# A relational graph layer: x in two 12-bit parts as fp32r words against masks spread to words by ScalarE, in place of three bf16 parts against fp8 masks

## What is computed

```python
rel_ids = jnp.arange(1, 5)                                  # four relations
masks = (relation[None] == rel_ids[:, None, None, None])    # relation is adj
h = jnp.einsum('rbnm,bmd->rbnd', masks, x)
y = jnp.einsum('rbnd,rdo->bno', h, weight) + bias           # weight (4,128,128)
out = layernorm(x + y, axis=-1)                             # eps 1e-5, no gain
```

## Time and profile before

| what | value |
|---|---|
| runs of the kernel | 136.88 us median of 3 (136.84 to 136.92) |
| the profiled execution's own time | 135.64 us |
| its span | 133.9 us |
| busy: PE, DVE, ACT, POOL | 119.4, 100.2, 78.4, 71.5 us |
| read from HBM, written to it | 37.88 MB, 4.19 MB |

### The profile page before, as it was taken

The page is one execution under the profiler, slowest core; times in us unless marked ns, Lnnn a source line. Parts: engine busy times, 40 slices in busy tenths (PEclk is TensorE's granted clock), DMA queues, the critical chain, the costliest instruction groups (busy, mean ns, idle before and its releaser), DMA issues.

```text
span 133.9 us, 2116 instructions
## 1 busy us (share of the span) xinstructions
PE 119.4 (89%) x675; PEld 73.2 (55%) x675; DVE 100.2 (75%) x274; ACT 78.4 (59%) x81; POOL 71.5 (53%) x79
## 2 busy tenths in 40 slices
PE   5884879949979999999999999999999999999920
PEld 4553668714526474746464646464656555567810
DVE  1487333177429999999999897969699999967871
ACT  3004862682699786959494949494949494123050
POOL 3000009950903995599379919990964559705260
PEclk9999999995999999999999999999999999999997
DMA  4999969999999999999999999999961200300322
GB/s 109 415 436 423 416 237 423 421 431 412 427 423 420 417 411 426 416 421 423 415 422 411 428 414 423 418 421 415 411 279 54 109 0 5 126 31 0 159 78 86
DMA packets 7788, 42.23 MB, mean 315 GB/s; under 512 B 864, under 2 KB 1376, under 8 KB 3936
## 3 DMA queue, kind: packets, MB, share of 16 engines
q1 hardware_dynamic: 7776, 42.08, 76.8%
HBM read 37.88 MB, written 4.19 MB: 314 GB/s over the span
## 4 chain that ended last, share of the span: by engine, by line
PE 63%; DMA 16%; ACT 5%; SPq 5%; DVE 5%; issue 2%; POOL 2%; POOLq 0%; DVEq 0%; ACTq 0%
PE h_ps L212 49%; DMA adj_sb<-in_adj_dram 16%; PE y_ps L219 9%; PE tp_ps L191 5%; ACT mask L183 4%; SPq L164 2%; POOL scale L237 2%; SPq L279 1%; DVE paired L492 1%; DVE stats L225 1%; SPq L167 1%; DVE total L509 1%; ACT h_sb L416 0%; DVE mean_var L230 0%; DVE out_sb L241 0%
## 5 line engine op out<-in xcount | busy, mean ns | idle before, releaser
L183 ACT ACTIVATE mask<-adj_sb 128x2048 fp8e3<-128x2048 int32 x30 | 55.9, 1902 | 14.3 <-DMA adj_sb<-in_adj_dram 14.3
L212 PE MATMUL h_ps<-maskT,x_sb 128*128 128x512 fp8e4 (+1 forms) x152 | 32.9, 359 | 3.5 <-DVE maskT L199 2.9
L212 PE MATMUL h_ps<-maskT,x_fine 128*128 128x512 fp8e4 (+1 forms) x152 | 32.0, 352 | 0.4 <-DVE x_fine L176 0.4
L212 PE MATMUL h_ps<-maskT,x_rest 128*128 128x512 fp8e4 (+1 forms) x152 | 32.2, 353 | 0.0
L179 POOL TENSOR_TENSOR x_bias<-x_sb,bias_sb 128x1024 f32<-128x1024 f32 x8 | 21.3, 2660 | 18.1 <-DMA bias_sb<-in_L_gnn_bias_dram 18.1
L199 DVE TENSOR_SCALAR maskT<-tp_ps 128x512 uint32<-128x512 uint32 x30 | 19.4, 683 | 11.4 <-PE tp_ps L191 11.4
L492 DVE SCALAR_TENSOR_TENSOR paired<-mask 128x512 uint32<-128x512 uint32 x13 | 20.3, 1562 | 6.6 <-ACT mask L183 6.1
L212 PEld LDWEIGHTS h_ps<-maskT,x_sb 128*128 128x128 bf16 x152 | 14.4, 97 | 19.0 <-DVE maskT L199 3.3
L356 POOL TENSOR_SCALAR minus_mean<-mean_var 128x4 f32<-128x4 f32 (+1 forms) x16 | 3.1, 195 | 37.2 <-DVE var_eps L234 21.4
L212 PEld LDWEIGHTS h_ps<-maskT,x_rest 128*128 128x128 bf16 x152 | 14.8, 98 | 11.5 <-DVE x_rest L173 0.3
L212 PEld LDWEIGHTS h_ps<-maskT,x_fine 128*128 128x128 bf16 x152 | 14.6, 96 | 11.8 <-DVE x_fine L176 0.7
(11 more groups left out here) (31 smaller groups left out, 63.8 us busy)
## 6 DMA issues: line engine op xcount, KB each, us to landing
adj_sb<-in_adj_dram SPq DMA_DIRECT2D x30, 1024.0 KB, 18.2
x_sb<-in_x_dram SPq DMA_DIRECT2D x8, 512.0 KB, 18.2
out_dram<-out_sb SPq DMA_DIRECT2D x7, 512.0 KB, 12.9
adj_sb<-in_adj_dram SPq DMA_DIRECT2D x4, 512.0 KB, 5.2
out_dram<-out_sb SPq DMA_DIRECT2D x1, 256.0 KB, 2.0
out_dram<-out_sb SPq DMA_DIRECT2D x2, 128.0 KB, 1.9
bias_sb<-in_L_gnn_bias_dram SPq DMA_DIRECT2D x1, 64.0 KB, 14.7
w_sb<-in_L_gnn_weight_dram SPq DMA_DIRECT2D x1, 64.0 KB, 14.5
```

The costliest lines, as they stand in the source:

```text
L183: nc.scalar.activation(mask[:, slot % NMASK].bitcast(code), adj_sb[:, slot % NADJ], ACT.Copy, scale=CODE, saturate=False).then_inc(done, 1)
L212: last = nc.tensor.matmul(h_ps[:, bank, 0:n], x_t, m_t, start=(part == 0 and t == 0), stop=(part == PARTS - 1 and t == TILES - 1))
```

## The change

- x is cut into two parts instead of three. `top` on VectorE masks x to its upper 12 significant bits (one `bitwise_and` over 1024 words); GpSimd copies that to the fp32r tile `x_hi`, and subtracts it from x into the fp32r tile `x_lo`. For batch 0 ScalarE makes the copy and VectorE the difference.
- The masks are fp32r words. VectorE makes the bytes of a unit (`convert`: min with 2, times 60, int32 to uint8, where 60 is the fp8e5 code of 1.0 and 120 that of 32768), TensorE transposes the words of every unit (no pairs), and ScalarE reads the four bytes of a word out of PSUM as fp8e5 and writes them as fp32r (`expand`, 2048 elements), with the sum of each row as a second result (`counts`), from which the flag is made in the end. The ORs, evacuations and pairs of VectorE are gone.
- The bias is no longer added to x. It is cut into three bf16 parts in three rows of a tile; one product of ones with that tile opens the accumulation of y (`spread_bias`), and the residual x is added straight from `x_sb`.
- The pieces of the first two units are gone; all units are whole, and h is copied unscaled. Four x slots (5 before), four `maskT` slots (6 before, four times as wide now). SP issues three small bias loads and the weight right after unit 1. 12 warm-up products, in bf16.

```diff
-        def convert_chunk(slot, done):
-            nc.scalar.activation(mask[:, slot % NMASK].bitcast(code), adj_sb[:, slot % NADJ], ACT.Copy, scale=CODE,
...
+        def take_top(x_slot, done):
+            nc.vector.tensor_scalar(flat(x_top[:, :]), flat(x_sb[:, x_slot]).bitcast(u32), TOP_BITS, None,
+                                    ALU.bitwise_and).then_inc(done, 1)
+        def take_lo(eng, x_slot, slot, done):
+            eng.tensor_tensor(flat(x_lo[:, slot]), flat(x_sb[:, x_slot]), flat(x_top[:, :]).bitcast(fp32),
+                              ALU.subtract).then_inc(done, 1)
+        def part_products(part, slot, places, bank, first, last_part):
+            n = (places.stop - places.start) * OP
             for t in range(TILES):
+                last = nc.tensor.matmul(h_ps[:, bank, 0:n], (x_hi, x_lo)[part][:, slot, t, :],
+                                        maskT[:, places, t // WORD, t % WORD, :],
+                                        start=(first and t == 0), stop=(last_part and t == TILES - 1))
...
+        def spread_bias(y, tiles):
+            n = tiles.stop - tiles.start
+            nc.tensor.matmul(y[:, 0:n, :], spread[:, :], bias_parts[:, 0:n, :], start=True, stop=False)
...
# SP
+            def load_batch(b):
                 if b >= NX:
+                    sp.wait_ge(added, CH * (b - NX + 1))
...
# POOL
             for b in range(B):
                 if b + 1 < B:
-                    rest(b + 1)
+                    hi(b + 1)
                 if b >= 1:
                     scales_half(2 * b - 1)
                 if b + 1 < B:
-                    fine(b + 1)
-                    bias_on(b + 1)
+                    lo(b + 1)
                 scales_half(2 * b)
...
# ACT
+            def expand(u):
+                act.wait_ge(turned, u + 1)
+                if u >= NMT:
+                    act.wait_ge(multiplied, u - NMT + 1)
+                nc.scalar.activation(maskT[:, u % NMT], turned_codes(u % NTP), ACT.Copy,
+                                     accum_out=counts[:, u:u + 1]).then_inc(expanded, 1)
...
+            for hf in range(HALVES - 1):
+                if hf >= 1:
+                    copy_half(hf - 1)
+                expand(2 * hf + 2)
+                expand(2 * hf + 3)
+                if hf >= 2:
+                    finish_half(hf - 2)
...
# DVE
+            def convert(u):
+                dve.wait_ge(adj_loaded[u % NADJ], 16 * (u // NADJ + 1))
+                if u >= NMASK:
+                    dve.wait_ge(turned, u - NMASK + 1)
+                nc.vector.tensor_scalar(mask[:, u % NMASK], adj_sb[:, u % NADJ].bitcast(u32), CAP, SET,
+                                        ALU.min, ALU.mult).then_inc(masked, 1)
...
+            for hf in range(HALVES - 1):
+                for u in (2 * hf + 5, 2 * hf + 6):
+                    if u < UNITS:
+                        convert(u)
+                if hf % 2 == 0 and hf // 2 + 1 < B:
+                    top(hf // 2 + 1)
+                if hf >= 1:
+                    add_half(hf - 1)
+                    measure_half(hf - 1)
+                if hf >= 2:
+                    finish_half(hf - 2)
...
# PE
+            turn(0)
+            turn(1)
             turn(2)
+            for hf in range(HALVES - 1):
+                if 2 * hf + 3 < UNITS:
+                    turn(2 * hf + 3)
+                hi_products(hf)
+                if 2 * hf + 4 < UNITS:
+                    turn(2 * hf + 4)
...
+                if hf >= 1:
+                    project_half(hf - 1)
+                lo_products(hf)
             products_quarter(HALVES - 1, 0)
             project_half(HALVES - 2)
+            products_quarter(HALVES - 1, 1)
             project_quarter(HALVES - 1, 0)
```

More of the change, by code:

```diff
@@ L13 @@
 CH = 4
[L14 to L19, removed]
+SET = 60.0
+CAP = 2.0
+FULL = 2048.5
+TOP_BITS = 0xFFFFF000
 def relational_layer(nc, x, adj, weight, bias, out):
-    fp32, bf16, fp8 = mybir.dt.float32, mybir.dt.bfloat16, mybir.dt.float8e4
-    code = mybir.dt.float8e3
-    i32, u32 = mybir.dt.int32, mybir.dt.uint32
+    fp32, fp32r, bf16 = mybir.dt.float32, mybir.dt.float32r, mybir.dt.bfloat16
+    code = mybir.dt.float8e5
+    i32, u32, u8 = mybir.dt.int32, mybir.dt.uint32, mybir.dt.uint8
     ALU, ACT, AX = mybir.AluOpType, mybir.ActivationFunctionType, mybir.AxisListType
@@ L218, in project @@
                 for r in range(relations):
[L219 to L220 removed]
+                    last = nc.tensor.matmul(y[:, n, :], h_of(r)[:, s], w_sb[:, r, :], start=False,
+                                            stop=(r == relations - 1 and s == tiles.stop - 1))
             last.then_inc(done, by)
@@ L456, in _ @@
                 with act.Fori(0, B) as b:
-                    with act.Fori(0, R) as r:
+                    for r in range(R):
                         for half in range(2):
+                            for ch in (2 * half, 2 * half + 1):
+                                k = CH * R * b + CH * r + ch
+                                act.wait_ge(g_turned, k + 1)
+                                if r > 0:
+                                    act.wait_ge(g_multiplied, 2 * R * b + 2 * r + half - 1)
+                                nc.scalar.copy(act_scratch[:, CH * r + ch + 1:CH * r + ch + 2], act_scratch[:, 0:1])
+                                nc.scalar.activation(maskT[:, ch], turned_codes(ch % NTP), ACT.Copy).then_inc(g_expanded, 1)
                             act.wait_ge(g_multiplied, 2 * R * b + 2 * r + half + 1)
@@ L496, in empty_pair @@
[L496 to L503 removed]
+            nc.vector.memset(act_scratch[:, :], 0.0).then_inc(scratch_set, 1)
@@ L504, in add @@
+            def add(b, y, tiles, count, by):
                 dve.wait_ge(projected, count)
-                dve.wait_ge(biased, b + 1)
-                if hf % 2 == 0 and b >= NTOTAL:
+                if b >= NTOTAL:
                     dve.wait_ge(act_normed, CH * (b - NTOTAL + 1))
-                tiles = slice(HT * (hf % 2) + O * c_slice.start, HT * (hf % 2) + O * c_slice.stop)
-                nc.vector.tensor_tensor(total[:, b % NTOTAL, tiles], y, x_bias[:, b % 2, tiles], ALU.add).then_inc(added, by)
+                nc.vector.tensor_tensor(total[:, b % NTOTAL, tiles], y, x_sb[:, b % NX, tiles], ALU.add).then_inc(added, by)
@@ new lines, in place_bias @@
+            def place_bias():
+                dve.wait_ge(bias_split, 3)
+                for q, part in zip(PARTS, (bias_rows, bias_rest, bias_fine)):
+                    last = nc.vector.tensor_copy(bias_parts[q:q + 1], upper(part[q:q + 1, :]).unsqueeze(1).to_broadcast(
+                        [1, HT, D]))
+                last.then_inc(bias_split, 1)
+            convert(0)
+            top(0)
+            convert(1)
+            dve.wait_ge(topped, 1)
+            take_lo(nc.vector, 0, 0, lo_made)
@@ L689, in products_quarter @@
                 place = (2 * hf + c) % NMT
-                wait_chunk(pe, piece_evacuated, evacuated, 2 * hf + c)
-                for part in range(PARTS):
-                    if hf % 2 == 0 and c == 0:
-                        x_ready(part, b)
-                    last = part_products(part, b % NX, b % 2, slice(place, place + 1), bank_of(hf, c))
-                last.then_inc(multiplied, 1)
+                pe.wait_ge(expanded, 2 * hf + c + 1)
+                part_products(0, b % 2, slice(place, place + 1), (hf + c) % NBANK, True, False)
+                part_products(1, b % 2, slice(place, place + 1), (hf + c) % NBANK, False, True).then_inc(multiplied, 1)
             def keep_warm(times):
```

443 lines of the change are left out of this document (145 added, 298 removed).

## The result

The changed kernel took 127.46 us, median of 4 runs (126.66 to 128.38); the kernel before took 136.86 beside it. The ratio is 0.9315, with the 95% interval [0.9244, 0.9385]: faster by 6.2 to 7.6%, and 6.3 us slower than the 121.2 predicted, inside its range. The execution that was profiled took 128.38 us, the longest of the four, 1.78 more than its span of 126.6.

The account below looks back on a forecast made before the run. TensorE was taken as the bound, at 5.82 us a half: start to 35.0, 11 halves to 99.0, end 19.2, span 118.2, plus 1.74 and 1.24 gave 121.2 us; range 116.5 to 130.

Parts of the forecast that it names:

- Rivals 3 and 4: Third: `convert` runs at the single rate, 143 us, chance 0.07. Fourth: an fp32r product still takes 427 ns, 167 us, chance 0.04.
- VectorE's own work: VectorE's operations per half without collisions, from two `convert` and half a `top` to the last normalisation: 5.44 us.
- VectorE against GpSimd: VectorE operations waiting out GpSimd's `lo`, expected at the second `convert` of odd iterations: 0.4 us a batch, bounds 0 and 1.9.
- TensorE with 0.08 for jostling: Pace of the late halves: TensorE's 5.74 us plus 0.08 for coupled engines, 5.82 us a half.
- Rival 1: Locks between VectorE and GpSimd, or ScalarE, set the pace: 7.0 us a half, 131 us; at 6.3, 126; chance 0.23.
- S14: Time TensorE starts half 14 (S with a number: start of that half), predicted at 99.0 us.
- S3: Time TensorE starts half 3, predicted at 35.0 us; from there halves were to follow 5.82 us apart.
- ScalarE and start: ScalarE 5.5 us a half, with `expand` 1.93; TensorE's first half begins at 15.8 us, 1.7 to 2 slower for its clock.
- the sign of being wrong: DMA, expected near 420 GB/s to 93 us: a dip would put SP's wait on the path.
- SP's new wait: A load of x waits for the sums of the batch four before; taken to cost nothing.
- End: From half 14's start on TensorE to the end of the span: 19.2 us with small waits, giving a span of 118.2.
- my own case: TensorE bounds the whole kernel: 5.65 to 6.1 us a half, 119.5 to 124.5 us, held at 0.57.

Follow-up runs that it names:

- E9: E6 with ScalarE normalising three of a half's four row tiles and VectorE one, up to half 11; 120.88 us.
- E1: The changed kernel with eps added to the variance on GpSimd instead of VectorE; 127.17 us.
- E7: The changed kernel with GpSimd making each `x_lo` of batches 1 to 7 twice, the first into a tile nobody reads; 138.56 us.
- E6: The changed kernel with TensorE's general loop over relations rolled again and ScalarE normalising a half one iteration later; 123.66 us.
- E8: The kernel before the change, with TensorE's general loop over four relations written as four copies; 139.27 us.
- E4: The changed kernel with TensorE's general loop, which doesn't run, looping over the relations again instead of four copies; 124.36 us.

## Why the prediction was right, and where it was wrong

The change is faster, as forecast, and the time lies in the range. The bound that the prediction named for the new kernel, TensorE, was wrong: it is VectorE with a stall behind GpSimd, and that the time came out near is in part luck.

**TensorE: right.** Eight fp32r products take 1.86 us, 233 ns each (230 taken); transposes 0.46, bias product 0.22, projection 0.89. Sum 2 x 1.86 + 2 x 0.46 + 0.22 + 0.89 = 5.75 (5.74 predicted), which is just the pace of E9. Rivals 3 and 4 fell: a convert is 1.22, an fp32r product far from 427. The Trainium skill (SBUF — State Buffer, "A bandwidth-pool intuition that's wrong") gives TensorE's moving operand 2 bytes a lane and cycle at 2.4 GHz, for bf16. An estimate from that figure puts 512 columns of 4-byte words at 427 ns; the measured 233 decides against this reading of it.

**VectorE's own work: right.** 5.44 a half predicted, 10.69 / 2 = 5.35 found.

**VectorE against GpSimd: the step that failed.** I took 0.4 us a batch for the collision and kept 0 and 1.9 as bounds; it is 1.32, in nearly every batch. Two things in it were wrong. `x_lo` was priced at the 1.90 of L176 but takes 2.40: it has two fp32 inputs, as the bias add of the kernel before has, whose mean was 2.66. And I looked for the collision at the converts only, arguing that they stand in line already. All but one do; the one that is hit is the small addition of eps before them, then by E1 and E7 the normalisation. 10.69 + 1.32 makes 6.0 a half against TensorE's 5.75, so the bound changed its engine: "TensorE with 0.08 for jostling" was the wrong mechanism with a number, 5.82, near the right 6.0. Rival 1, that the locks set the pace, was the right one in its milder form: with 6.3 a half it gave S14 at 104 and 126 us. (Its 109 to 110 for 7.0 a half is a slip, 35.0 + 11 x 7.0 is 112.)

**The other way round, L550 was the right guide.** GpSimd's short power never stretched a convert, so rival 1 in its full form (7.0 a half) did not come. But I costed GpSimd at 1.5 for a half's scales, "it bounds nothing", and did not ask what its wait does to those behind it: a power took 3.3 to 3.9 us with two or three double-rate operations of VectorE beside it, so `shift` was late, ScalarE waited 19.8 us for it, and an expand behind that came later. E6 puts this at 1.2 us.

**What it adds up to at S14**, +5.4: 0.4 at S3; 2.0 for pace (5.5 batches of 12.0 instead of 11.64); and 3.0 more between S3 and S7, at 62.4, where a half took 6.75 rather than 6.0. Of these 3.0, 1.2 fall on the first half alone, 35.40 to 42.63, where TensorE waits for a convert of VectorE (TensorE, then VectorE):
```profile
42.63 0.74 PE L178 MATMUL tp_ps<-identity,mask 128*128 128x128 f32 x4 [0.73 <-DVE mask L426]
```
```profile
41.36 2.36 DVE L426 TENSOR_SCALAR mask<-adj_sb 128x2048 uint8<-128x2048 uint32 x2
```
That convert stands in VectorE's order behind a `top`, an add, statistics and a normalisation, from 38.05 on. The loads had let TensorE work 2.65 us ahead of VectorE's `top` (35.4 against 38.05), and I had not counted that this lead must be given back once VectorE sets the pace; by S7 TensorE stood 0.5 behind (62.4 against 61.88), where it stayed. E9 has this first half too (35.29 to 42.39) and then goes on at 5.8. Another 1.2 is ScalarE's order (E6). The last 0.6 stays open.

**ScalarE and start: right.** Expand 1.87 (1.93 taken), the row sum an instruction of its own of 197 ns, mostly overlapped (0.1 taken); reading every fourth byte cost nothing; `hi` 1.04 (1.5 taken). The start came within 0.4 us, with the granted clock at 0.50, the 1.2 GHz level, from 10.3 to 20.5 us, after TensorE had little to do from 7 us on; I had put 1.7 to 2 us on the first half for it, and the loads covered it.

**DMA: the sign of being wrong came, its cause was another.** I had said that a dip would put SP's new wait on the path. There are dips, to 365, 359 and 281 GB/s in single slices, and 400 in the mean. But they go when VectorE gets less to do, with the same four x slots: E9 has 420 in the mean and, but for the first and the last slice of the loads, none under 404, while E6, which differs from it in that alone, still dips to 341 and 320. So they follow from a late VectorE, which frees the slots.

**End: a term was missing.** From S14 to the last normalisation 16.8 for 16.6. (The terms given add up to 13.8 + 5.5 = 19.3, and the prediction has 19.2 with small waits; it matters little.) Then 5.4 instead of 2.6, as the branch takes 4.05 us where it took 0.37. The line was in the diff; I read it as code that doesn't run. Code that doesn't run had a price of 2.6 us in E8; in E4 2.7 of the 4.0 that the span lost are of the end.

**The sum.** The span was 126.6 for 118.2 predicted, +8.4: 5.4 at S14, 0.2, and 2.8 for the branch. The profiled execution was 0.9 above the median where I had put it 1.24 below, which by chance takes 2.1 back: 6.3 in the time. With the loop rolled (E4) the kernel stands at 124.3, inside the 119.5 to 124.5 of my own case, but with VectorE as the bound and not TensorE.

## What to carry to other kernels

Where VectorE and GpSimd both work out of SBUF, add to VectorE's own sum that part of each long GpSimd operation under which VectorE has no statistics to take (1.3 of 2.4 us here, 2.2 of the second 2.4 in E7), and give a short GpSimd operation in a chain the length of VectorE's run beside it. When several engines have within some 7% of the same work, ask which one gets the stalls, since that one is the bound: here one of VectorE's two normalisations of a half, moved to ScalarE, was worth 2.8 us, and 16 us of waiting taken from ScalarE 1.2. And read a diff for what it does to code that is jumped over.

## What the runs showed of the hardware

- Between VectorE and GpSimd it does not only count which began first. A GpSimd operation over 1024 elements (2.40 us) holds up VectorE operations even of 4 elements a lane (0.17 to 1.48) or the normalisation (0.59 to 2.77 for two). VectorE's statistics ran under it at their usual 0.87 and 0.38 for four. A GpSimd power of 4 elements, begun 0.11 to 0.13 us ahead of a convert, doesn't hold it up (2.35 for two, as ever) and takes 3.33 beside two and 3.94 beside three, where alone it takes 1.07. The Trainium skill (SBUF — State Buffer, "Who interferes with whom") gives the ports to whichever starts first; the long `x_lo` agrees with that, the short power does not. It may be that a GpSimd operation asks for the ports only some time after its start in the records; no run here tells.
- A branch over a loop body written four times instead of once took 3.7 us more on TensorE's queue (0.36 to 4.05 and 0.37 to 4.09), though nothing there is executed.
- fp32r products of 512 columns took 233 ns each at the clock of 1.00, back to back, 7 more than the 226 of bf16 against fp8 in the kernel before; one column a cycle at 2.4 GHz would be 213, so they pass once.
- A ScalarE read of every fourth byte of PSUM into 4-byte words took 1873 ns for 2048, no more than the 1.93 us worked out for fp32 from the earlier trace rows.
